# Four heads' scores side by side in 32 rows each, three score buffers in six banks, one value bank and one job bank, and a branch that holds a whole attention

## The reference, cut to what matters

```python
def ffn(x):        # w complex, 256 x 256
    return real(ifft(fft(x) @ w)) + bias

def attn(x):       # 16 heads, Dh = 8, scale = 4; only the left 128 columns
    left = x[..., :128]
    q, k, v = (left @ W.T for W in (Wq, Wk, Wv)), each (N, S, 16, 8)
    energy = einsum('nqhd,nkhd->nqkh', q, k)
    att = softmax(energy / scale, axis=2)
    return einsum('nqkh,nkhd->nqhd', att, v).reshape(N, S, 128) @ Wo.T + bo

x = x + 0.5 * ffn(layernorm(x))
x = x + attn(layernorm(x))
x = x + 0.5 * ffn(layernorm(x))
```

## Time and profile before

| | us |
|---|---|
| median of 3 runs | 363.37 |
| lowest and highest | 362.71, 365.26 |
| the profiled execution, its own time | 364.46 |
| its span, first to last instruction | 362.7 |
| mean granted TensorE clock | 0.995 |

### The profile page before, as it was taken

One profiled execution on the slowest core, in us unless ns is written; L12 is line 12 of the kernel. 1 busy time (PEld: TensorE's weight loads), 2 busy tenths in 40 slices (PEclk: granted clock), 3 DMA queues, 4 the chain that ended last, 5 costly groups with the idle time before them and its releaser, 6 DMA issues.

```text
span 362.7 us, 8793 instructions
## 1 busy us (share of the span) xinstructions
PE 346.3 (95%) x3446; PEld 136.7 (38%) x3446; DVE 178.5 (49%) x494; ACT 252.4 (70%) x266; POOL 109.5 (30%) x104
## 2 busy tenths in 40 slices
PE   8876999899999999999999999999999999999986
PEld 6533333224433343333433443334333433233323
DVE  3655257465436753575346644666255521423155
ACT  2002677678778777788787777787777888888741
POOL 6442126151612432150614252052411160006004
PEclk9999899999999999999999999999999999999999
DMA  7624649907901385129901693229412780100001
GB/s 223 191 98 142 120 177 201 214 36 183 233 23 66 128 175 164 42 87 195 213 9 61 174 174 122 68 102 175 74 38 82 160 138 12 59 2 0 31 29 60
DMA packets 19573, 40.61 MB, mean 112 GB/s; under 512 B 3620, under 2 KB 6052, under 8 KB 18564
## 3 DMA queue, kind: packets, MB, share of 16 engines
q1 hardware_dynamic: 18404, 38.76, 43.5%
q10 hardware_dynamic: 1120, 1.18, 1.1%
HBM read 26.63 MB, written 12.58 MB: 108 GB/s over the span
## 4 chain that ended last, share of the span: by engine, by line
PE 88%; ACT 4%; issue 3%; DVE 2%; DMA 2%; ACTq 0%; POOL 0%; DVEq 0%
PE ot L669 33%; PE misc L580 24%; PE scores L649 22%; ACT probs L531 3%; PE misc L589 2%; PE scores L547 2%; PE misc L621 1%; PE scores L554 1%; DMA QS<-q_scr 1%; DMA q_scr<-qp 1%; PE scores L562 1%; PE ot L580 0%; PE misc L634 0%; ACTq L288 0%; PE scores L589 0%
## 5 line engine op out<-in xcount | busy, mean ns | idle before, releaser
L531 ACT ACTIVATE probs<-scores 128x1024 f32<-128x1024 f32 x256 | 247.2, 1022 | 77.3 <-PE scores L649 77.3
L669 PE MATMUL ot<-probs,VS 128*32 128x512 f32 x1024 | 138.3, 608 | 1.7 <-issue 1.4
L649 PE MATMUL scores<-QS,KS 34*128 34x512 f32 x512 | 98.1, 453 | 4.9 <-ACT probs L531 3.9
L649 PEld LDWEIGHTS scores<-QS,KS 34*128 34x128 f32 x512 | 41.0, 184 | 68.5 <-ACT probs L531 50.9
L429 POOL TENSOR_SCALAR veps<-mv 128x4 f32<-128x4 f32 (+1 forms) x25 | 5.7, 227 | 185.0 <-DVE mv L781 185.0
L836 DVE SCALAR_TENSOR_TENSOR x_out<-misc,rstd,x_out 128x256 f32<-128x256 f32 x32 | 15.5, 483 | 49.5 <-PE misc L580 49.5
L669 PEld LDWEIGHTS ot<-probs,VS 128*32 128x32 f32 x1024 | 20.3, 108 | 45.6 <-issue 44.3
L580 PE MATMUL misc<-half_ffn,xT 128*32 128x256 f32 x512 | 33.2, 379 | 0.2 <-ACT xT L535 0.2
L580 PE MATMUL misc<-half_ffn,xT_in 128*32 128x256 f32 x480 | 31.3, 384 | 1.3 <-DVE half_ffn L939 1.3
L811 DVE SCALAR_TENSOR_TENSOR x<-misc,rstd,x_in 128x256 f32<-128x256 f32 x24 | 11.6, 484 | 39.2 <-PE misc L580 39.1
L831 DVE TENSOR_TENSOR x<-misc,x 128x256 f32<-128x256 f32 x32 | 13.5, 420 | 30.4 <-PE misc L580 30.4
(11 more groups left out here) (83 smaller groups left out, 240.3 us busy)
## 6 DMA issues: line engine op xcount, KB each, us to landing
KS<-k_scr SPq DMA_DIRECT2D x60, 128.0 KB, 4.8
QS<-q_scr SPq DMA_DIRECT2D x60, 128.0 KB, 4.7
x_in<-x SPq DMA_DIRECT2D x8, 512.0 KB, 6.6
xT_in<-x_t SPq DMA_DIRECT2D x8, 512.0 KB, 7.5
k_scr<-kp SPq DMA_DIRECT2D x8, 512.0 KB, 2.7
q_scr<-qp SPq DMA_DIRECT2D x7, 512.0 KB, 3.3
out<-x_out SPq DMA_DIRECT2D x14, 256.0 KB, 2.1
q_scr<-qp ACTq DMA_DIRECT2D x1, 512.0 KB, 3.3
```

The source lines that it names most:

```text
L531: nc.scalar.activation(probs[u % PRING][:, :, :], scores[u % 2][:, :, :], ACT.Exp, scale=SCORE_SCALE).then_inc(exp_done, 1)
L649: last = mm(scores[u % 2][:, i, :], KS[b % 2][rows, slot, kt * P:(kt + 1) * P].bitcast(F32R), QS[b % 2][rows, slot, :].bitcast(F32R), star ...
L669: last = mm(ot[g][COL * j:COL * (j + 1), :], VS[b % 2][:, kt, h, :], probs[(2 * s + j // 2) % PRING][:, j % 2, :], start=s % 8 == 0, stop= ...
```

## The change

- Scores: the shift rows go, each head has 32 rows, and four heads stand in the four groups of 32 partitions (`LANES` = 4, `place`). `score_quad` runs four matmuls one behind the other and signals once. Three buffers of two banks (`SRING` = 3); quad s+1 waits until the exponential 2s has been taken.
- Banks: six for scores, one `ot` (its transposition is pulled out of `normalize` as `take_values`, in slots 7 and 15), one `misc`. In the prologue the first jobs, and in the epilogue the last, use score banks too. A job waits until all jobs of earlier slots have been evacuated.
- Jobs: WO in two pieces instead of four, and the tables written anew, mostly one job in a slot. Guard in slot 12.
- Guard: the branch body computes the whole attention of the batch exactly (`guard` in place of `maxima`): for each of 64 head tiles one score matmul, four transposes and four fp32 products with the values, and the output product. No shift, no shift DMAs. Its condition and the skipping are as before.
- Prologue: no early tiles of batch 1, `keep_parts` replaced by `keep_awake(18)`, and 16 `keep_awake` behind the guard. K and Q rows come in DMAs by lane (4 lanes x 2), for batch 0 one slot's worth first.
- POOL and VectorE orders are moved accordingly.

```diff
-SROW = TERMS * Dh
-ROWS = SROW + PARTS
-SIDES = 2
+ROWS = TERMS * Dh
+LANES = P // ROWS
+SLOTS = H // LANES
+SRING = 3
...
+STEADY = {0: [("F1_0", 2)], 1: [("QT", 1)], 2: [("WO_0", -1)], 3: [("WO_1", -1)], 4: [("T3_0", -1)], 5: [("T3_1", -1)],
+          6: [("F1_1", 2)], 7: [("F1_2", 2)], 8: [("V", 1)], 9: [("F1_3", 2), ("N", 1)], 10: [("F2_0", -1), ("NT", 1)],
+          11: [("F2_1", -1)], 12: [("F2_2", -1)], 13: [("LT", 2)], 14: [("KT", 2)], 15: [("F2_3", -1)]}
+BEGIN = {0: [("F1_0", 1)], 1: [("F1_1", 1)], 2: [("F1_2", 1)], 3: [("F1_3", 1)], 4: [("F1_0", 2)], 5: [("F1_1", 2)],
+         6: [("LT", 1)], 7: [("KT", 1)], 8: [("QT", 1)], 9: [("V", 1)], 10: [("F1_2", 2), ("N", 1)],
+         11: [("F1_3", 2), ("NT", 1)], 14: [("LT", 2)], 15: [("KT", 2)]}
+GUARD_SLOT = 12
...
+                for lane in range(2):
+                    k_rows(sp, 0, slice(0, 1), lane, first_rows_in)
                 sp.wait_ge(q_stored, 16)
+                for lane in range(2):
+                    q_rows(sp, 0, slice(0, 1), lane, first_rows_in)
...
+            def k_in(b):
+                wait(sp, quad_done, QUADS * (b - 1))
+                sp.wait_ge(k_stored, 16 * (b + 1))
+                for lane in range(LANES):
+                    k_rows(sp, b % 2, slice(0, SLOTS), lane, rows_loaded)
...
+            for u in range(PAIRS * B):
+                act.wait_ge(scores_ready, u // 2 + 1)
+                wait(act, quad_done, (u - PRING) // 2 + 1)
+                nc.scalar.activation(probs[u % PRING][:, :, :], scores[u % SRING][:, :, :], ACT.Exp,
+                                     scale=SCORE_SCALE).then_inc(exp_done, 1)
...
-                wait(pe, evacuated, n - 1)
+                if n <= INDEX["NT", 0]:
+                    wait(pe, evacuated, n - 3)
+                elif not (b == B - 1 and name[:2] in ("WO", "F2")):
+                    pe.wait_ge(evacuated, slot_jobs(name, b)[0])
...
+            def score_quad(b, s):
+
+                _, _, kt, heads = quad_units(s)
...
+                u = PAIRS * b + 2 * s
+                wait(pe, exp_done, u + 2 - SRING)
+                for j, h in enumerate(heads):
+                    lane, slot = place(h)
+                    rows = slice(ROWS * lane, ROWS * (lane + 1))
+                    last = mm(scores[(u + j // 2) % SRING][:, j % 2, :], KS[b % 2][rows, slot, kt * P:(kt + 1) * P].bitcast(F32R),
                               QS[b % 2][rows, slot, :].bitcast(F32R), start=True, stop=True)
                 last.then_inc(scores_ready, 1)
...
+            def guard(b, taken):
+
+                pe.wait_ge(guard_step, GUARD_STEPS * (b + 1))
                 small = pe.value_load(safe[0:1, 0:1], min_val=0, max_val=1)
                 with pe.If(small == 0):
...
                     for t in range(T):
+                        for first in range(0, H, GROUP):
+                            heads = range(first, first + GROUP)
+                            for h in heads:
...
+                                mm(misc[:, :], QS[b % 2][rows, slot, t * P:(t + 1) * P].bitcast(F32R),
+                                   KS[b % 2][rows, slot, :].bitcast(F32R), start=True, stop=True).then_inc(exact_ready, 1)
...
+                            for h in heads:
+                                pe.wait_ge(exact_taken, taken)
+                                for kt in range(T):
+                                    last = nc.tensor.transpose(misc[:, kt * P:(kt + 1) * P],
+                                                               exact[:, h - first, kt * P:(kt + 1) * P], ident[:, :])
...
+                                for kt in range(T):
+                                    last = mm(misc[:, 0:COL], exactT[:, kt * P:(kt + 1) * P], VS[b % 2][:, kt, h, :],
+                                              start=kt == 0, stop=kt == T - 1)
...
+                        nc.tensor.transpose(misc[:, 0:P], attn[:, :], ident[:, :]).then_inc(exact_ready, 1)
+                        pe.wait_ge(exact_taken, taken + 1)
+                        mm(misc[:, 0:E], attnT[:, :], wo_sb[:, :], start=True, stop=True).then_inc(exact_ready, 1)
...
                 with pe.Else():
+                    pe.sem_inc(exact_ready, EXACT_MM)
...
+            keep_awake(18)
             pe.wait_ge(ident_loaded, 16)
...
             keep_awake(8)
+            guard(0, evac_count("NT", 0))
+            keep_awake(16)
             pe.wait_ge(consts_set, 7)
+            score_quad(0, 0)
...
+                    if s == 7:
+                        take_values(it, 0)
+                    if s == 15:
+                        take_values(it, 1)
                     run_jobs(it, s)
+                    if s == 8:
+                        normalize(it, 0)
+                    if s == 15 and it + 1 < B:
+                        normalize(it, 1)
...
+                        if s == 5 and it + 3 < B:
+                            norm0_stats(it + 3, range(0, 2))
+                        if s == 6 and it + 3 < B:
+                            norm0_stats(it + 3, range(2, T))
+                            norm_moments(0, it + 4)
+                        if s == 11 and it + 2 < B:
+                            left_half(it + 2)
```

More of the change, by code:

```diff
@@ L469, in _ @@
             rstd_of(0, 2)
+            pool.wait_ge(late_loaded, 32)
+            begin_x2(0)
+            next_x(2)
             rstd_of(1, 2)
@@ L554, in keep_awake @@
                     mm(bank, waking[:, 0:P], waking[:, :], start=True, stop=True)
-            def keep_parts(n, rows):
-                zeros = waking[:, :].bitcast(F32R)
-                for _ in range(n):
-                    for r in range(P // rows):
-                        part = slice(rows * r, rows * (r + 1))
-                        mm(scores[r // 2][:, r % 2, 0:S // 2], zeros[part, 0:P], zeros[part, :], start=True, stop=True)
             pe.wait_ge(waking_set, 1)
@@ L629, in job @@
                     pe.wait_ge(sq_done, 2 * (b + 1))
-                    mm(bank[0:32, :], head_ones[:, 1, :], sq_q[:, :], start=True, stop=True)
-                    last = mm(bank[32:64, :], head_ones[:, 0, :], sq_k[:, :], start=True, stop=True)
+                    for j in range(4):
+                        half = slice((j % 2) * E, (j % 2 + 1) * E)
+                        last = mm(bank[COL * j:COL * (j + 1), E:2 * E], head_ones[:, 1 - j // 2, :],
+                                  (sq_k if j // 2 else sq_q)[:, half], start=True, stop=True)
@@ L760, in _ @@
             job("WO_1", B - 1)
[L761 to L768 removed]
+            for i in range(2):
+                last_transposes(i)
+            for t in range(T):
+                job(f"F2_{t}", B - 1)
         @block.vector
@@ L1010 @@
     for h in range(H):
-        side, slot = place(h)
-        heads[HEADS * side + slot] = h
+        lane, slot = place(h)
+        heads[SLOTS * lane + slot] = h
     by_head = (heads[:, None] * Dh + np.arange(Dh)[None, :]).ravel()
```

544 lines of the change are left out of this document (253 added, 291 removed), and 4 rows, old and new, of the table STEADY.

## The result

The changed kernel takes 387.7 us (median of 4 runs, 385.2 to 392.6), the kernel before 363.6 beside it (362.7 to 365.3): a ratio of 1.064, 95% interval 1.056 to 1.072. The forecast was 356.5, in a range of 343 to 366: wrong in size and in sign. The interval leaves out the 392.6, an execution more than 1.5% above the fastest. The profiled span is 384.8 us against a sum of 356.2.

The account below looks back on a forecast made before the run. TensorE, busy 95%, was taken as the bound; prologue 38.9, iteration 0 37.2, five of 37.3, then 34.2, 30.9, tail 13.1 and guards 15.4 summed to 356.2, scaled to 356.5 us, range 343 to 366.

Parts of the forecast that it names:

- Scores: In each slot, four 32-row matmuls cost one pass; score part 0.66 to 0.44, full-job slot 2.52 to 2.30 us.
- rival 4: The four score matmuls do not overlap with real operands: 28 us more, 385 us; chance 0.02.
- The change of tile shape: Stands before the score pass with the first weight load, and stays within the 0.44 us forecast.
- Jobs and one bank: Steady iteration: slots sum to 36.6 us, waits for single job and value banks add 0.75, giving 37.3 against 39.8.
- The guard: TensorE's jump over the long never-taken body must fetch its target: 2.2 us visible in iterations 0 to 6, 15.4 in all.
- M: Code-fetch stall at TensorE's guard branch: 2.9 us, of which 2.2 shows after the sequencer's lead hides 0.7.
- rival 3: TensorE's clock falls to half at the guard, some 1.7 us more each; span 372, or 368 with M = 2.9; chance 0.10.
- its stall runs beside TensorE's: At the guard, VectorE's jump over some 500 instructions stalls in parallel with TensorE, before it must empty slot 13's LT.
- Prologue: First value quad at 38.9 us instead of 36.4, with a 2.9 us guard stall and 16 keep_awake matmuls before first scores.
- Iteration 0: First iteration takes 37.2 us instead of 42.7, with 0.5 for late rows and 0.9 for waits.
- more 16 KB instruction packets: Sign of the guard's fetch: more code packets than the 32 in the earlier trace; no number given.
- first rival: No fetch stall at the guard, or one hidden within the sequencer's lead: span 339, 340 us; chance 0.15.

Follow-up runs that it names:

- b_1700: Kernel before, with 773 more matmuls in TensorE's never-taken branch, so the jump goes over about 1,700 instructions: 403.6 us, ratio 1.104.
- b_388: Kernel before, with 120 more matmuls in TensorE's never-taken branch, so every jump goes over 388 instructions: 391.3 us.
- n_dve: Kernel after, with only VectorE's guard body left out; TensorE still jumps over its own: 384.8 us, ratio 1.053.
- pad_fix: hint_fix with never-run instructions padding the never-taken bodies, 24 idle instructions at VectorE's start and TensorE's announcements from b = 2 at slot 10: 350.1 us, ratio 0.960.
- n_pe: Kernel after, with only TensorE's guard body left out; VectorE still jumps over its own: 360.2 us, ratio 0.989.
- hint0: Kernel after, both guard bodies kept, with the branch targets announced ahead of the guards: 364.6 us.
- hint_fix: Kernel after, with branch targets announced earlier than in hint0 for TensorE's b = 0, 1 and VectorE, and the two orders of n_fix: 363.4 us, ratio 0.997.
- n_fix: Kernel after without guard bodies on TensorE and VectorE, with rstd_of(1, 3) ahead of next_x(3) and batch 1's Q ahead of K: 351.1 us, ratio 0.965.

## Why the prediction was wrong, step by step

- **Scores: right.** 2.30 from load to load, ScalarE idle 0.37 for 0.36 forecast. Four 32-row matmuls cost what one pass costs, and rival 4 is out: in the slot shown the four start within 0.01 us (146.515 to 146.525), and the first value matmul starts 0.44 after the first of them, the 0.44 forecast. "The change of tile shape" in that 0.44 was not shown by itself. What the trace has is the distance between starts where one shape follows another: 0.33 from the job's last four matmuls to the scores (148.481 to 148.81), against 0.22 from four to four within the job.
- **Jobs and one bank: right.** The steady iteration without bodies is 37.1 where 37.3 was forecast; F1_3 with N 2.41, F2_0 with NT 2.49, slots with transposes 2.0 to 2.1. Iteration 7 (31.6 for 30.9), the tail (14.3 for 13.1) and iteration 6 (35.2 for 34.2) are each about 1 us above.
- **The guard: the right place and sign, mis-sized.** "Its target cannot be the next packet, and must be fetched" is what b_1700 and b_388 show: where the jump passes two boundaries or more, from b = 2 on, the branch takes 3.3 to 3.7 us, and a packet starts 0.9 to 1.0 us into it. The term that failed is M: 2.9, of which 2.2 was to be seen. The visible stall is 3.1, so M is 3.8 in the forecast's own terms (the branch itself takes 3.4 to 4.0 in the trace). That is 0.9 x 7, 6 us. The packets' records say what M lacked. In the kernel after a packet starts 0.9 to 1.5 us into each branch and takes 0.9 to 1.4: with the 2.0 to 2.5 us until it has landed the forecast's 2.9 was ample. But the branch ends only 1.3 to 1.5 us after the landing, and for that last part the sum had no term.
- **The clock: what turned the sign.** The forecast said that rival 3 decides from M = 3.5; at 3.8 it did. "A stall of 2.2 beside dense work is less idle than that" rested on the M that was too small, and set it at 0.10: around the guard of iteration 1 TensorE was busy 0.70 of 3.60 us, less than the 1.24 of 3.40 in the earlier trace rows that had been followed by a fall. Why the fall came at five of the seven guards inside the iterations and not at the other two stays open. Its price was mis-sized too: 2.8 us an iteration with what goes with it, against 1.7, as half clock lasts 6.8 us here and 3.4 in the earlier trace rows. By the rival's sum with M = 3.8 the span is 356.2 + 7 x 1.7 + 7 x 0.9 = 374; the span was 384.8.
- **VectorE: "its stall runs beside TensorE's" holds only in part.** Alone it costs 1.3 us an iteration. Under TensorE's it is nearly hidden (n_dve is 2.9 us faster than the kernel after).
- **Prologue: 42.5 for 38.9.** TensorE stands 5.16 us at the first guard, not 2.9, and then about six of the 16 `keep_awake` run at half clock, 0.42 us apart (4.51 us for 15). In the kernels whose first branch on TensorE is quick the first value quad comes at 37.3 to 39.0.
- **Iteration 0: overlooked.** "Moving begin_x2, next_x and the statistics keeps every POOL and VectorE product a slot or more ahead of its user" was false for rstd_of(1, 3), and "K and Q rows ... hidden" for batch 1's. Without bodies it is 46.6 where 37.2 was forecast. In the kernel after both lie under the guard.
- The packets went as forecast ("more 16 KB instruction packets": 45 for 32). The 32 packets of the earlier trace rows, which the forecast held against its first rival, decide nothing: at 256 instructions each, 31.4 packets hold the 8,044 that it counted, so they say that the code came in once and whole, which it would with a stall at a jump and without one. What speaks against that rival are the branches, 3.4 to 4.0 us in the kernel after, and the packet within each.

## What to carry to other kernels

Code that never runs can have a price if a branch jumps over it; here it cost 34.5 us of 388. Count its instructions (an fp32 matmul was four here) and ask whether the target is beyond the next packet (256 instructions on TensorE in these runs, 128 on VectorE by my estimate). If the body can't be made short, announce the target ahead of a packet boundary and pad the body that never runs so that the target stands early in its packet, as in pad_fix (branches of 0.3 to 0.4 us, 350.1 us in all). Where TensorE is the bound, price a stall of 3 us with a fall of the clock behind it, about as much again (3.1 and 2.8 us an iteration here); the fall came at five of the seven guards inside the iterations.

## What the runs showed of the hardware that was not expected

- A jump beyond the next packet holds TensorE's branch 3.3 to 3.7 us from b = 2 on, over 388 instructions (b_388, b = 2, 3 and 7) as over 1,694 (b_1700). VectorE's jump over some 500 holds it 2.7 to 3.1 (n_pe).
- An announced target helped where the engine passed a packet boundary between announcement and branch (hint0 on TensorE, b = 2 to 6: 0.4 to 1.2 us), and not elsewhere (b = 0 and 1: 3.75 and 3.76), with one exception. For VectorE one boundary position explains all eight cases in hint_fix, and pad_fix, laid out by it, has eight quick ones of eight. The b = 7 of hint0 on TensorE, and of hint_fix at the same place, was quick (0.43 us) without such a boundary in my count, though the packet is there (hint0: 304.28 to 305.42, the branch at 306.89), and stays unexplained.
- Four VectorE instructions of 1.12 us took 3.14 beside a POOL addition of 2.45 (n_fix), and 3.16 in pad_fix. Why they slow each other is not shown.
